# Attention with normed queries on one Trainium2 core: raw scores and row maxima head by head in alternating banks, in place of pairs of heads through both banks

## The reference, cut to what matters

```
q, k, v = split(x @ Wqkv.T + bqkv)          # per head: 256 x 8
q = q / sqrt(mean(q*q) + 1e-6) * wq         # k likewise, with wk
attn = softmax(q @ k.T)                     # no scale, no mask: 256 x 256 per head
x = x + (attn @ v) @ Wo.T + bo
```

## Time and profile before

| | |
|---|---|
| median of 2 runs | 2665.68 us (2663.59 to 2667.76) |
| the profiled execution's own time | 2664.31 us |
| its span, first to last instruction | 2662.5 us |
| PE busy | 2038.3 us (77%) |
| DVE busy | 1468.7 us (55%) |
| ACT busy | 1096.7 us (41%) |
| POOL busy | 1139.9 us (43%) |
| mean granted TensorE clock | 0.840 of full |

### The profile page before, as it was taken

The page is one execution under the profiler, slowest core; times in us unless marked ns, Lnnn a source line. Parts: engine busy times, 40 slices in busy tenths (PEclk is TensorE's granted clock), DMA queues, the critical chain, the costliest instruction groups (busy, mean ns, idle before and its releaser), DMA issues. The chain is left out here.

```text
span 2662.5 us, 44455 instructions
## 1 busy us (share of the span) xinstructions
PE 2038.3 (77%) x14950; PEld 1417.9 (53%) x14950; DVE 1468.7 (55%) x4368; ACT 1096.7 (41%) x2495; POOL 1139.9 (43%) x1761
## 2 busy tenths in 40 slices
PE   7885788878778667877858888699914888878992
PEld 6764767667664223334424554488811444437881
DVE  5996655655457533435747667443324767754332
ACT  2332233232334346555415554454401666564440
POOL 4452222222134545553455564725345445352534
PEclk9997888888798768788868988799965878689996
DMA  7000000000000000000000000156710000015673
GB/s 231 1 0 1 1 1 1 0 0 0 0 1 0 0 1 1 1 1 1 0 0 2 2 2 2 46 163 203 212 52 0 2 1 1 1 33 171 196 224 85
DMA packets 93920, 109.21 MB, mean 41 GB/s; under 512 B 12944, under 2 KB 76832, under 8 KB 93600
## 3 DMA queue, kind: packets, MB, share of 16 engines
q1 hardware_dynamic: 85536, 89.96, 11.0%
q0 software_dynamic: 8192, 16.79, 2.3%
HBM read 78.14 MB, written 28.57 MB: 40 GB/s over the span
## 5 line engine op out<-in xcount | busy, mean ns | idle before, releaser
L1502 DVE TENSOR_REDUCE a2mx<-PS 128x4 f32<-128x1024 f32 x128 | 156.0, 1218 | 68.0 <-PE PS L1683 67.3
L1938 ACT ACTIVATE a2prob<-PS 128x512 f32<-128x512 f32 x256 | 144.9, 600 | 98.4 <-PE PS L1707 98.3
L1502 DVE TENSOR_REDUCE a1mx<-PS 128x6 f32<-128x768 f32 x128 | 122.2, 955 | 77.7 <-PE PS L1690 77.2
L488 POOL TENSOR_TENSOR la_qc<-la_q,k_cosF 128x512 f32<-128x512 f32 x32 | 40.8, 1276 | 270.6 <-ACT la_q L688 270.6
L295 PE MATMUL PS<-cv_rT,cv_diag 128*128 128x256 f32 x640 | 148.6, 393 | 4.8 <-ACT cv_rT L343 4.8
L1941 ACT ACTIVATE a0prob<-PS 128x1024 f32<-128x1024 f32 x128 | 127.1, 1026 | 49.4 <-PE PS L1707 49.1
L1938 ACT ACTIVATE a1prob<-PS 128x384 f32<-128x384 f32 x256 | 114.1, 496 | 78.8 <-PE PS L1707 78.7
L1347 POOL TENSOR_SCALAR_AFFINE_SELECT a1prob<-a1prob 128x256 f32<-128x256 f32 x256 | 97.4, 409 | 99.9 <-ACT a1prob L1938 98.7
L295 PEld LDWEIGHTS PS<-cv_rT,cv_diag 128*128 128x128 f32 x640 | 125.7, 198 | 24.4 <-ACT cv_rT L343 4.2
L524 DVE TENSOR_TENSOR la_kv<-PS,k_bkv 128x512 f32<-128x512 f32 x64 | 44.3, 692 | 148.8 <-PE PS L607 148.8
L255 DVE SCALAR_TENSOR_TENSOR cv_y<-cv_gl,k_conv_w,cv_y 128x256 f32<-128x256 f32 x224 | 117.2, 596 | 0.0
(11 more groups left out here) (521 smaller groups left out, 5652.0 us busy)
## 6 DMA issues: line engine op xcount, KB each, us to landing
m1awr<-in_wtab SPq DMA_DIRECT2D x46, 514.0 KB, 3.7
m1bwr<-in_wtab SPq DMA_DIRECT2D x46, 514.0 KB, 3.8
rows_in<-cv_blank SPq DMA_DIRECT2D x46, 128.0 KB, 2.2
m1axin<-rows_in SPq DMA_DIRECT2D x46, 128.0 KB
rows_out<-m1ayo SPq DMA_DIRECT2D x46, 128.0 KB, 1.9
m1bxin<-rows_in SPq DMA_DIRECT2D x46, 128.0 KB
rows_out<-m1byo SPq DMA_DIRECT2D x46, 128.0 KB, 2.0
X<-in_x SPq DMA_DIRECT2D x4, 512.0 KB, 6.2
```

The costliest lines, as they stand in the source:

```text
L1502: v.tensor_reduce(mx[:, 2 * j:2 * j + 2, :], MB[:, :, 0:SEG * seg_len].rearrange("p h (s n) -> p h s n", n=seg_len), AX.X, ALU.max).then_i ...
L1938: act.activation(prob[:, h % RING, 0:n_prob], SB[(b * NH + h) % NSB][:, 0:n_prob], ACT.Exp, scale=scale).then_inc(s["exp"], 1)
```

## The change

For the attention that isn't causal, `W` is 1: `prepare_top` and `prepare_max` handle one head, in bank h mod 2, at each of the 16 values of h in place of each even one. `prepare_top` waits for the maxima of head h - 2, the last that used the same bank. For the causal attention `W` is 2 and the instructions and waits stay as they were. Nothing else moves in any stream.

```diff
+    W = 2 if causal else 1
+    TOPS = NH // W
...
             def take_q(b):
                 if keep_max:
-                    finished(v, s["top"], (b - 1) * PAIRS - 1)
+                    finished(v, s["top"], (b - 1) * TOPS - 1)
...
             def prepare_max(b, j):
-                v.wait_ge(s["top"], b * PAIRS + j + 1)
-                v.tensor_reduce(mx[:, 2 * j:2 * j + 2, :],
-                                MB[:, :, 0:SEG * seg_len].rearrange("p h (s n) -> p h s n", n=seg_len), AX.X,
+                v.wait_ge(s["top"], b * TOPS + j + 1)
+                bank = MB[:, :, 0:SEG * seg_len] if W == 2 else MB[:, j % 2:j % 2 + 1, 0:SEG * seg_len]
+                v.tensor_reduce(mx[:, W * j:W * j + W, :], bank.rearrange("p h (s n) -> p h s n", n=seg_len), AX.X,
                                 ALU.max).then_inc(s["mx"], 1)
 
             def prepare_minus(b, half):
...
-                v.wait_ge(s["mx"], b * PAIRS + (half + 1) * PAIRS // 2)
+                v.wait_ge(s["mx"], b * TOPS + (half + 1) * TOPS // 2)
...
             def step(b):
                 for h in range(NH):
-                    if keep_max and h % 2 == 0 and b + 1 < B:
-                        prepare_max(b + 1, h // 2)
+                    if keep_max and h % W == 0 and b + 1 < B:
+                        prepare_max(b + 1, h // W)
...
             if keep_max:
-                for j in range(PAIRS):
+                for j in range(TOPS):
                     prepare_max(0, j)
-                    if j == PAIRS // 2:
+                    if j == TOPS // 2:
                         take_q(1)
...
-                finished(pe, s["mx"], b * PAIRS + j - 1)
+                finished(pe, s["mx"], b * TOPS + j - (1 if W == 2 else 2))
                 for t in range(NT):
                     keys = (t + 1) * P if causal else N
-                    for i in range(2):
-                        h = 2 * j + i
+                    for i in range(W):
+                        h = W * j + i
                         rows = slice(lane(h), lane(h) + KEYED)
-                        last = pe.matmul(MB[:, i, t * seg_len:t * seg_len + keys],
+                        last = pe.matmul(MB[:, i if W == 2 else h % 2, t * seg_len:t * seg_len + keys],
...
                 for h in range(NH):
                     if h % 2 == 0:
                         scores(b, h // 2)
-                        if b + 1 < B:
-                            prepare_top(b + 1, h // 2)
+                    if h % W == 0 and b + 1 < B:
+                        prepare_top(b + 1, h // W)
                     group(b, h)
...
-                for j in range(PAIRS):
+                for j in range(TOPS):
                     prepare_top(0, j)
-                    if j == PAIRS // 2 - 1:
+                    if j == TOPS // 2 - 1:
```

## The result

The changed kernel took 2748.06 us (2746.30 and 2749.81, two runs) against 2665.68 us: 82 us more, a ratio of 1.030 with a 95% interval of 1.027 to 1.0331. The prediction, 2700 us with a range to 2722, had the direction and not the size.

The account below looks back on a forecast made before the run. No engine was taken as saturated; a ring of waits over POOL sets full-clock steps, PE bounds half-clock stretches. 15.6 + 13.5 + 1 + 7 - 2.2 = +35 us on 2664.3 gave 2699, median 2700 us; forecast 2680 to 2718, range 2655 to 2722.

Parts of the forecast that it names:

- rival 2: Maxima and raw scores bound the steps, so alternating banks removes up to 35.8 us of waits: 2650 us, chance 0.05.
- the ring over POOL: Aggregate, POOL's chain, prepare_hi, prepare_raw, complete_ot, aggregate: a closed loop of waits setting full-clock steps, 17.9 us.
- Matmuls without partners: Raw scores on PE: one head's two matmuls follow one another, costing as much as a pair, 0.32 us.
- Halved reduces: Maxima on DVE: a pair costs 1.20 us in place of 1.14, 8 us more of DVE over 128 pairs.
- A: From prepare_raw's end to the aggregate: odd heads behind waits make it 1.2 us later, +15.6 us in 13 steps.
- B: Head 5's raw scores behind the projection delay complete_ot: +1.5 us in 9 half-clock steps, 13.5 us; full clock +1.
- C: Unpartnered raw scores between scores at h = 14 and the projection, at half clock: 0.8 us in 9 steps, +7.
- D: Waits for maxima that go before step 0: about 13 us in place of 15.1, -2.2 us.
- Rival 4: New waits before complete_ot and head 11's raw scores halve the mid-step clock, about 5 us 5 times: 2725, chance 0.14.
- The check that the prediction set: The forecast counts as wrong if the clock in the steps differs from 0.78 by over 0.05.

Follow-up runs that it names:

- e1: Changed kernel with both heads of a pair placed together at even h, on PE and DVE; ratio 0.999 to the kernel before.
- e10: e1's version with statistics and aggregate moved from h = 11 to 9 and root from h = 15 to 13; ratio 0.9992.
- e11: Kernel before with statistics and aggregate moved from h = 11 to 9 and root from h = 15 to 13; ratio 0.9994.
- e3: Kernel before with the four raw-score matmuls of a pair issued head by head in the same place; ratio 1.0023.
- e2: Kernel before with only the reduce of a pair split into two instructions, one for each bank; ratio 1.0015.
- e6: Changed kernel with 8 unread matmuls issued on PE in the wait before complete_ot, no wait removed; ratio 1.0183.
- e12: Kernel before with four small reduces of a constant on DVE ahead of prepare_raw in each a2 step; ratio 1.0076.
- e14: e1's version with 8 unread matmuls in each of two PE waits, at h = 2 and before the router's turns; ratio 0.9974.
- e15: Kernel before with 8 unread matmuls in each of two PE waits, at h = 2 and before the router's turns; ratio 0.9986.

## Why the prediction was wrong

*What bounds the kernel.* That no engine is saturated and that removed waits for maxima would bring nothing was right: with the same alternation and no bad placement (e1) the ratio is 0.999. So rival 2 gives nothing that can be told from no change. The Trainium skill's rule on rotating through PSUM banks (Perfetto Trace Analysis, Matmuls) agrees with e1's trace as far as the waits go, 7.3 us in place of 20.3; in time it brought nothing here. That the ring over POOL was what full-clock steps wait for was claimed too surely: e10 and e11 loosened it without effect. And it was read from one step: `prepare_hi` waits for POOL in 5 of the twelve steps before, and in 2 (1.2 us in all) of the changed kernel's.

*Matmuls without partners.* Right in kind. e3 prices the packing in the same place at 6 us.

*Halved reduces.* Right: 0.60 us apart (2225.81, then the next instruction 0.60 later), and e2 finds no cost that can be measured.

*A.* Right in place and nearly in size where the clock is full. In the changed kernel's third step the aggregate stands at

```profile
2115.83 0.25 DVE L1457 BATCH_NORM_AGGREGATE a2mv<-a2st 128x2 f32<-128x6 f32 x2
```

8.08 us behind `complete_ot` (8.07 in e6), before 7.05: +1.0 for 1.2. The turns and the products are 2.83 us apart, for 2.7. But in the step at 2213.89, at half clock, `complete_ot` to the aggregate is 10.09 us.

*B.* Right at half clock: from the projection's start to `complete_ot` 5.13 us, before 3.83, so 1.3 for 1.5.

*C.* Counted at 7 us for the half-clock stretches that existed; there are now more of them, 12 of 13 steps in place of 9. No run shows this term by itself.

*D.* Right: from the first maxima of sequence 0 (2037.90, now 2039.58) to the first `prepare_minus` (2052.98, now 2052.65) it is 15.1 us before and 13.1 after, for 15.1 and about 13.

*The step that failed* is the one that the sum took without a term: every stretch was costed at the clock that it had before. What the runs showed instead is a clock of 0.65 where 0.79 had been, in the twelve steps. The working with its clock unchanged agrees in sum with e6, where the clock is 0.80: twelve steps of 293.8 us are 32 more than the 261.6 of the kernel before (of another chip), close to the 34 or so that A, B and C come to in twelve steps. That is partly luck, since the fills take PE time of their own. The changed kernel adds another 32 to 40 us in the same steps, at 0.64 to 0.65. Rival 4 named this mechanism, a lower clock behind the gap before `complete_ot`, but looked for it in the middle of the step alone, 5 times, and gave it 0.14. The turns are slow in about that many steps, 3 or 4; what it left out is that the half-rate stretch that had ended ahead of `complete_ot` now takes it in as well, in 6 of 11 steps, and that three more projections are at half clock. The check that the prediction set, a clock within 0.05 of 0.78, is the one that fired.

*Not settled:* why the clock falls so far. It isn't the missing partners (e3), and one delay alone takes it to 0.73 (e12). Filling one gap brings its mean back (e6). But the gap alone doesn't decide a step: the waits of 1.61 us at 2107.75 and at 2219.02 are alike, and turns of 1.07 us follow the one, of 1.89 the other. That leaves the sum of several gaps in a step, with PE late enough for each slow stretch to lengthen the step; this is argued from the runs, not shown by one.

## What to carry to other kernels

In a hand-ordered stream, splitting an instruction in two is also a decision about where the second half is queued. If it lands behind work that takes long or waits (here a projection, transposes and a copy), the engines wait for each other in places where the whole instruction never did. With both halves where the whole one stood, the same split cost nothing here (0.999, against 1.030 or 1.024).

A gap on PE is to be priced twice where PE is near the path: by its length, and by the matmuls behind it at half clock. A forecast that adds gaps should ask for the stretch behind each whether it would stay at its level, and whether the engine is near the path there: in e14 and e15 a clock of 0.86 and more was worth next to nothing.

## What was not expected of the hardware

Eight matmuls whose results nobody reads, put into a wait, made the steps of the changed kernel faster: twelve of them take 293.8 in place of 333.5 us, at a clock of 0.80 in place of 0.64 (ratio of the whole 1.0183 in place of 1.0242). The gaps at issue were short, 1.4 to 1.6 us once a step before `complete_ot`, with PE busy for 88% of the time. And the same kind of fill in the kernel before raised the clock as well, 0.79 to 0.86, for at most 0.3% of time.
